# Dense weights split once into DRAM, gate's input normalized once, no POOL in the dense part, and the denominator's floor as a positive part on ScalarE

## The reference

```python
decay = exp(-exp(w)) * (0.5 + 0.5 * tf)          # per channel and batch
ek = exp(min(k, 30)); ekv = ek * v                # k and v are both the side input
nf, df = scan(ekv), scan(ek)                      # a = a * decay + in, forward
nb, db = the same, backward
euk = exp(min(u + k, 30))
num = nf + nb - ekv + euk * v
den = df + db - ek + euk
out = sigmoid(r) * (num / max(den, 1e-8)) * (0.8 + 0.2 * tf)

x = x + (out0(x) @ (weight * scale).T + bias)     # layer 0
c = out1(x)                                       # layer 1
flat = rmsnorm(c) * norm_w
top 4 of softmax(flat @ router_w.T), renormalized
routed = sum over the 4 of weight * (silu(flat @ w1g) * (flat @ w1u)) @ w2   # per expert
shared = (silu(flat @ sg) * (flat @ su)) @ sd
x = x + c + routed + shared
```

## Time and profile before

| | |
|---|---|
| three runs | 5500.07, 5501.99, 5503.63 us |
| profiled execution | 5515.08 us |
| its span | 5513.1 us, 61940 instructions |
| TensorE busy (PE) | 4469.8 us, 81% |
| VectorE busy (DVE) | 3139.4 us, 57% |
| ScalarE busy (ACT) | 1907.9 us, 35% |
| POOL busy | 1923.7 us, 35% |
| moved by DMA | 649.34 MB, mean 118 GB/s |

### The profile page before, as it was taken

The page is one execution under the profiler, slowest core; times in us unless marked ns, Lnnn a source line. Parts: engine busy times, 40 slices in busy tenths (PEclk is TensorE's granted clock), DMA queues, the critical chain, the costliest instruction groups (busy, mean ns, idle before and its releaser), DMA issues.

```text
span 5513.1 us, 61940 instructions
## 1 busy us (share of the span) xinstructions
PE 4469.8 (81%) x19471; PEld 3552.8 (64%) x19473; DVE 3139.4 (57%) x2812; ACT 1907.9 (35%) x2587; POOL 1923.7 (35%) x1350
## 2 busy tenths in 40 slices
PE   0036786868777787997459999999999999999998
PEld 0014555655555565765348888878878887888887
DVE  8889898988989896445222323434343214324232
ACT  2234444434444444442212223333343214223232
POOL 0023748475656657554721111111111111111111
PEclk9998888989888888998779999999999999999999
DMA  1123342424333334345433444545564435445352
GB/s 59 53 84 99 108 137 106 145 96 134 109 125 113 116 118 136 119 132 75 135 82 104 107 107 117 180 123 175 151 194 148 107 61 175 122 105 149 89 163 57
DMA packets 248186, 649.34 MB, mean 118 GB/s; under 512 B 44720, under 2 KB 110704, under 8 KB 223472
## 3 DMA queue, kind: packets, MB, share of 16 engines
q1 hardware_dynamic: 200224, 489.21, 26.0%
q0 software_dynamic: 47824, 158.43, 13.9%
HBM read 500.69 MB, written 146.87 MB: 117 GB/s over the span
## 4 chain that ended last, share of the span: by engine, by line
PE 53%; issue 2%; POOL 2%; DVE 1%; DMA 1%; ACT 0%; DVEq 0%; POOLq 0%; ACTq 0%; SPq 0%
PE ps L1273 30%; PE ps L1287 15%; PE ps L1174 4%; PE ps L1254 2%; POOL slots_dram L477 2%; PE ps L1262 1%; DMA slots_dram<-work 1%; PE ps L1192 0%; PE ps L1190 0%; DMA work<-slots_dram 0%; POOL halves L212 0%; DVE work L890 0%; DVE work L887 0%; DVE work L886 0%; POOL work L223 0%
## 5 line engine op out<-in xcount | busy, mean ns | idle before, releaser
L1174 PE MATMUL ps<-halves 128*128 128x512 f32 x6144 | 1606.3, 424 | 713.0 <-POOL halves L257 352.3
L1174 PEld LDWEIGHTS ps<-halves 128*128 128x128 f32 x6144 | 1249.5, 205 | 1066.7 <-issue 439.1
L1273 PE MATMUL ps<-halves 128*128 128x512 f32 x7152 | 1745.6, 397 | 27.5 <-DVE halves L1102 22.1
L1273 PEld LDWEIGHTS ps<-halves 128*128 128x128 f32 x7152 | 1328.9, 189 | 300.9 <-DVE halves L1102 24.3
L212 POOL TENSOR_TENSOR halves<-work,halves 128x1024 fp32r<-128x1024 f32 x239 | 694.9, 2909 | 675.7 <-ACT halves L598 675.4
L1287 PE MATMUL ps<-halves 128*128 128x512 f32 x3576 | 835.0, 389 | 1.3 <-DVE halves L1112 1.3
L1287 PEld LDWEIGHTS ps<-halves 128*128 128x128 f32 x3576 | 671.4, 188 | 140.5 <-DVE halves L1112 1.5
L1097 DVE TENSOR_TENSOR halves<-ps,halves 128x1024 fp32r<-128x1024 f32 x150 | 183.7, 1225 | 876.1 <-ACT halves L696 876.1
L459 POOL COPY add_idx<-work 128x1 int32 x149 | 27.0, 181 | 1692.1 <-DVE work L1118 1692.1
L1102 DVE TENSOR_TENSOR halves<-work,halves 128x1024 fp32r<-128x1024 f32 (+1 forms) x320 | 440.3, 1435 | 109.8 <-ACT halves L705 109.8
L696 ACT ACTIVATE halves<-ps 128x1024 fp32r<-128x1024 f32 x150 | 153.9, 1026 | 960.7 <-PE ps L1273 849.3
(11 more groups left out here) (163 smaller groups left out, 4582.0 us busy)
## 6 DMA issues: line engine op xcount, KB each, us to landing
work<-expert_w SPq DMA_DIRECT2D x192, 1024.0 KB, 5.5
work<-shared_w SPq DMA_DIRECT2D x256, 512.0 KB, 4.4
work<-side_t SPq DMA_DIRECT2D x33, 512.0 KB, 3.4
work<-x_t SPq DMA_DIRECT2D x33, 512.0 KB, 4.1
gated_dram<-work SPq DMA_DIRECT2D x32, 512.0 KB, 3.0
ratio_dram<-work SPq DMA_DIRECT2D x32, 512.0 KB, 2.9
work<-gated_dram SPq DMA_DIRECT2D x64, 256.0 KB, 2.7
work<-x_t SPq DMA_DIRECT2D x64, 256.0 KB, 3.2
```

What stands on the lines that cost most here:

```text
L1174: last = pe.matmul(bank(k % 4), w[k % 2][:, c * P:(c + 1) * P], op[:, part], start=(c == 0 and w is piece_hi and op is hi), stop=(c == CB ...
L1273: last = pe.matmul(ps_h[:, a * 512:a * 512 + 512], xp[:, xk * P:(xk + 1) * P], wp[:, rhs], start=(xk == 0 and xp is xhi and wp is whi), st ...
```

## The change

- Units 0 to 7's time also carries a split of the 32 weight pieces: SP loads four a unit, ScalarE writes the high part, TensorE computes piece minus high part in PSUM by two fp32 products (identity by piece, negative identity by high part), ScalarE copies it out as the low part, and SP stores both to `split_dram` (1 MB a piece). The eighth group runs behind unit 6, ahead of unit 7, without a unit of its own; then SP waits for all stores and loads the first three pieces.
- A product loads both parts as two 512 KB halves (each with the high and low part of four blocks of the contraction), in four slots, three pieces ahead. There is no split of weights in the halves.
- C1 is kept for all eight blocks. The sum of squares comes at step `step_l(o)` + 1. R is made at step 16, and Z = C1 x norm weight x R for all eight blocks there, with its split, transposes and logits; gate's and up's outputs need no factor then, nor do the experts. Rows are stored by one DMA of 2 MB per half.
- The low parts of z, c and the activation are made by VectorE; POOL keeps only fills, entries, gathers and adds.
- In the unit: the numerator's forward scan comes before the denominator's backward scan; the two edge products go to ScalarE; the floor becomes `Relu(den - low)` on ScalarE, and `low` is added back as the bias of Ln and in the first refining step.

The diff, cut to its core (SP's waits of the input loads, the declarations of tiles and the routing's index changes are left out):

```diff
+SLOTS = 4
+AHEAD = SLOTS - 1
...
-        def with_halves(eng, unit, fill, tail, loop_q=UNITS_PER_HALF):
+        def with_halves(eng, unit, fill, tail, alone, weights=lambda: None):
             with eng.Fori(0, 2 * UNITS_PER_HALF - 1) as u:
-                unit(u, nothing, alone=True)
+                unit(u, lambda i: alone(u, i))
+            last = 2 * UNITS_PER_HALF - 1
+            for i in range(FILLS_PER_UNIT):
+                alone(last, i)
+            weights()
             unit(2 * UNITS_PER_HALF - 1, lambda i: fill(-1, STEPS - FILLS_PER_UNIT + i, first=False, prev=False, next_=True))
...
+            def load_piece(h, k, step):
+                for j in range(2):
+                    wait(sp, "chunk" if j == 0 else "product", h * STEPS + (k - SLOTS + 1))
+                    sp.dma_start(piece[k % SLOTS][j].bitcast(i32), split_dram[(2 * step + j) * P:(2 * step + j + 1) * P, :])\
+                        .then_inc(piece_sem[k % SLOTS][j], 16)
...
+            def alone(u, i):
+                m = i // 2
+                if i % 2 == 0:
+                    sp.wait_ge(s["split_pe"], u * 4 + (m + 1))
+                    sp.dma_start(raw_w[m], shared_w[ds((u * 4 + m) * P, P), :]).then_inc(raw_sem[m], 16)
+                else:
+                    sp.wait_ge(s["split_lo"], u * 4 + (m + 3))
+                    sp.dma_start(split_dram[ds((u * 4 + m) * (2 * P), 2 * P), :].rearrange("(j p) c -> p j c", p=P),
+                                 split_w[m].bitcast(i32).rearrange("p (j c) -> p j c", j=2)).then_inc(split_sem[m], 16)
+            def weights():
+                for m in range(4):
+                    sp.wait_ge(split_sem[m], 8 * 16 + 1)
+                for k, i in first_half[:AHEAD]:
+                    load_piece(0, k, i)
...
-                if not final(h) or i <= FIRST_RANK:
-                    low_halves(pool, h, i, first, prev, next_)
...
-            split_piece_lo(pool, 0, 0)
-            with_halves(pool, unit, fill, lambda: None)
+            fill(HALVES - 2, 2, first=False, prev=True, next_=True)
+            fill(HALVES - 1, FIRST_RANK + 1, first=False, prev=True, next_=False)
...
+                def edges(l):
+                    at = ds(u + l * BLOCKS, 1)
+                    sc.wait_ge(s["h_fwd"], u * 2 + l + 1)
+                    sc.activation(edge_in[:, 0:1], F[:, SEQ - 1:SEQ], ACT.Copy, scale=edge[:, at]).then_inc(s["h_edge"], 1)
+                    sc.wait_ge(s["nf"], u * 2 + l + 1)
+                    sc.activation(edge_in[:, 1:2], G[:, SEQ - 1:SEQ], ACT.Copy, scale=edge[:, at]).then_inc(s["n_edge"], 1)
...
                 def inverse(l):
+                    sc.wait_ge(s["h_all"], u * 2 + l + 1)
+                    sc.activation(F, F, ACT.Relu, bias=neg_low[:, at]).then_inc(s["den"], 1)
                     sc.wait_ge(s["den"], u * 2 + l + 1)
-                    sc.activation(G, H, ACT.Ln).then_inc(s["g_ln"], 1)
+                    sc.activation(N, F, ACT.Ln, bias=low[:, at]).then_inc(s["g_ln"], 1)
                     sc.wait_ge(s["g_ln"], u * 2 + l + 1)
-                    sc.activation(G, G, ACT.Exp, scale=-1.0).then_inc(s["g_inv"], 1)
+                    sc.activation(N, N, ACT.Exp, scale=-1.0).then_inc(s["g_inv"], 1)
...
-            def split_piece(h, k):
+            def alone(u, i):
+                m = i // 2
+                if i % 2 == 0:
+                    sc.wait_ge(raw_sem[m], (u + 1) * 16)
+                    sc.wait_ge(split_sem[m], u * 16 + 1)
+                    sc.activation(split_part(m, 0), raw_w[m].rearrange("p (j c) -> p j c", j=2), ACT.Copy).then_inc(s["split_hi"], 1)
+                else:
+                    sc.wait_ge(s["split_pe"], u * 4 + (m + 5))
+                    sc.activation(split_part(m, 1), ps[m % 2][:, :].rearrange("p (j c) -> p j c", j=2), ACT.Copy)\
+                        .then_inc(s["split_lo"], 1)
...
+            def normalize(h):
+                ve.wait_ge(s["sums"], h * CB + CB)
+                ve.tensor_scalar(SQ, SUM_BANK, 1.0 / CH, 1e-6, ALU.mult, ALU.add).then_inc(s["mean"], 1)
+                ve.wait_ge(s["r_exp"], h + 1)
...
+                ve.scalar_tensor_tensor(R, SG, 1.5, R, ALU.add, ALU.mult).then_inc(s["r_set"], 1)
+                for o in range(CB):
...
+                    ve.scalar_tensor_tensor(Z[o % 2], C1[o], nrm[:, o:o + 1], R, ALU.mult, ALU.mult).then_inc(s["z"], 1)
+                    if o:
+                        split_z_lo(h, o - 1)
+                split_z_lo(h, CB - 1)
...
+            with pe.Fori(0, 2 * UNITS_PER_HALF) as u:
+                for m in range(4):
+                    pe.wait_ge(s["split_hi"], u * 4 + (m + 1))
+                    pe.wait_ge(s["split_lo"], u * 4 + (m + 1))
+                    for j in range(2):
+                        part = slice(j * HALF, (j + 1) * HALF)
+                        pe.matmul(ps[m % 2][:, part], ident[:, :], raw_w[m][:, part], start=True, stop=False)
+                        last = pe.matmul(ps[m % 2][:, part], neg_ident,
+                                         split_w[m][:, 2 * j * HALF:(2 * j + 1) * HALF].bitcast(f32), start=False, stop=True)
+                    last.then_inc(s["split_pe"], 1)
...
+            def square_sums(h, o):
+                pe.wait_ge(s["sq"], h * CB + (o + 1))
+                pe.matmul(SUM_BANK, ones[:, :], SQ, start=(o == 0), stop=(o == CB - 1)).then_inc(s["sums"], 1)
...
-                        if i == step_l(o) + 2:
-                            by_token(h, o)
+                        if i == step_l(o) + 1:
+                            square_sums(h, o)
...
+                    if i == 2 * CB - 1:
+                        for o in range(CB):
+                            by_token(h, o)
```

More of the change, by code:

```diff
@@ L305, in _ @@
                 sp.sem_inc(s[name], 1)
+            for done in split_sem:
+                sp.sem_inc(done, 1)
+            sp.sem_inc(s["split_pe"], 4)
+            sp.sem_inc(s["split_lo"], 2)
             sp.dma_start(ww[:, :], w_all).then_inc(s["cond_in"], 16)
@@ new lines, in _, with next_piece, load_cl @@
+            first_half = [(k, i) for i, k in products(0, True)]
+            def next_piece(h, k, first, next_):
+                ahead = k + AHEAD
+                if ahead < STEPS - CB:
+                    load_piece(h, ahead, dict(first_half)[ahead] if first else ahead + CB)
+                else:
+                    load_piece(h, ahead, ahead - (STEPS - CB) if next_ else step_d(ahead - (STEPS - CB)))
+            def load_cl(h, c):
+                rows, cols = half_rows(h, c)
+                if c < 2:
+                    wait(sp, "c1", (h - 1) * CB + (CB - 2 + c + 1))
+                else:
+                    wait(sp, "c_lo", h * CB + (c - 1))
+                sp.wait_ge(s["gated_out"], ((h // 2) * CB + (c + 1)) * 16 + 1)
+                sp.dma_start(RL[c % 2], gated_dram[rows, cols]).then_inc(rl_sem[c % 2], 16)
@@ L379, in store_out, with unit @@
                 sp.dma_start(to, RS.rearrange("p (t c) -> p t c", c=P)).then_inc(s["o_out"], 16)
-            def unit(u, fill, alone=False):
+            def unit(u, fill):
                 fill(0)
@@ L407, in _ @@
             load_x(0)
-            for k, src in first_half[:2]:
-                load_piece(0, k, src)
-            with_halves(sp, unit, fill, tail)
+            with_halves(sp, unit, fill, tail, alone, weights)
             def load_weights(j):
@@ L584, in unit @@
                 fill(3)
+                fill(4)
+                edges(1)
                 euk(1)
-                fill(4)
                 fill(5)
@@ L614, in out_copy, with rows_copy @@
                 sc.activation(RS, OUT_BANK, ACT.Copy).then_inc(s["o_copy"], 1)
+            def rows_copy(h, o):
+                sc.wait_ge(s["z_tr"], h * CB + (o + 1))
+                sc.activation(ZROWS[:, :, o * P:(o + 1) * P], Z_BANK.rearrange("p (t c) -> p t c", t=HT), ACT.Copy)\
+                    .then_inc(s["z_copy"], 1)
             def fill(h, i, first, prev, next_):
+                if prev and i == 0:
+                    act_hi(h - 1, CB - 1)
                 if not before_all(h):
-                    if any(i == a for a, _ in products(h, first)):
-                        split_piece(h, number(i, first) + 1)
                     for o in range(CB):
@@ L709, in silu @@
                 sc.wait_ge(s["a_tr"], g * 2 + 1)
-                apart(sc)
-                sc.activation(act[:, a * 256:a * 256 + 256], ps_h[:, a * 512:a * 512 + 256], ACT.Silu,
-                              scale=gains[:, ds(g + GT, 1)]).then_inc(s["silu_done"], 1)
+                sc.activation(act[:, a * 256:a * 256 + 256], ps_h[:, a * 512:a * 512 + 256], ACT.Silu).then_inc(s["silu_done"], 1)
             def split_act(g, a):
@@ L1069, in fill @@
+                if next_:
+                    for c in range(CB):
+                        if i == STEPS - CB + c:
+                            split_c_lo(h + 1, c)
                 if final(h, HALVES - 2) and i == 0:
@@ L1164, in product @@
```

(15 more changed lines are left out.)

485 lines of the change are left out of this document (213 added, 272 removed).

## The result

| | median | lowest to highest | ratio to before |
|---|---|---|---|
| before | 5502.81 us | 5500.07 to 5504.36, 4 runs | |
| after | 5616.16 us | 5613.68 to 5618.67, 4 runs | 1.0207, 95% interval 1.0189 to 1.0224 |

The change costs 113 us; 5434 with a range of 5320 to 5545 was predicted. The profiled execution of after took 5613.68 us, span 5612.0.

A forecast was written before the change was run, and what follows sets the result against it. VectorE was taken to bound halves 1 to 5. Terms 133 + 72 - 182 - 30 - 30 - 7.5 - 24 = -68.5 took the profiled 5515.08 to 5446.6; less 13.1 for the median, 5434 us, range 5320 to 5545.

The forecast's parts named there:

- the walk through the queues in halves 1 to 5: Halves 1 to 5, queues followed unit by unit: 262 us a half against 298.4, -182 in all.
- two squares behind inverses: Steps 0 to 7 of a half: two squares queued behind inverses on ScalarE, three cold products, 62.0 us.
- C1 at 9.8: Steps 8 to 15: C1 done 9.8 us after VectorE starts reading the fifth lin product, the square at 12.2.
- two sums and 14 products to 96: Half 6, its first two products already done: this stretch ends at 96 us; the half takes 211 against 241.3, -30.
- Rival 1: Halves: handshake on the squares and late 1 MB pieces cost more, 285 us a half, total +66, 5568 us; chance 0.19.
- Rival 2: Halves: scans fall in with the waits, VectorE's pace of 235 us a half, total -216, 5286 us; chance 0.12.
- Rival 3: Units 0 to 6: splits hide beside units at 42 to 44 us, loads running ahead, total 5308 us; chance 0.05.
- The units beside splits: Units 0 to 6 with four serial weight splits each: 61.6 instead of 42.1 us a unit, +133 in all.
- Unit 6 with the eighth group and unit 7: Before the halves: unit 61.6 us, then eighth weight group 73.9 and unit 7 47.8, together 121.7 instead of 49.4, +72.
- The routing: Half 7: starts 143 us in against 147.0 and takes 37.5 instead of 41 us, -7.5.
- the wait of rows 8: Before the puts: second slot fill landed 24 us after entries were ready; emptying slots earlier removes it, -24.
- The floor: Scan units: Relu on ScalarE frees 64 x 0.75 = 48 us of VectorE; taken alone the move would be 24 us worse.

The follow-up runs named there:

- four edits: Changed kernel with sums one step later, a group's four loads together, ScalarE's high part of the next input first, floor back on VectorE: 5133.78 us, ratio 0.9331.

## Why the prediction was wrong

**The step that failed** is the walk through the queues in halves 1 to 5, at the sentence "the sum of squares now follows one product earlier, and TensorE stands until ScalarE's square of it". The mechanism was named; it was followed at too few places. Its four parts, in pairs that need no common boundary: steps 24 to 31 and 0 to 7 were put at 67.0 + 62.0 = 129 and took 54.1 + 91.3 = 145; steps 8 to 15, 65.3 against 68.9; steps 16 to 23, 66.4 against 68.5. That is 22 us a half over the walk's 260.7. The prediction had "two squares behind inverses" there; the trace has the read of the first lin product behind three scans, its sigmoid behind the exponential and sigmoid of x, and 12.7 us of TensorE standing. That is a chain of the kind that was worked out for the fifth lin product, at a place where it was not looked for. The second part is the order on VectorE. The prediction let C1 follow the sigmoid at once ("C1 at 9.8"), but in the code the read of the down product stands before it, and so the sum always comes after that product. The run with C1 first has the order that was assumed, and it parts the two: its steps 8 to 15 take 65.2 us, the predicted 65.3, while its steps 24 to 31 and 0 to 7 stay some 10 us over the 129. So about 10 us a half are the order on VectorE, and about 10 stay in the stretch with the chain ahead of the first sum.

**It was then not carried on.** For half 6 the prediction took "two sums and 14 products to 96": seven pairs without a stop. The pairs took 14.6 and 16.2 us in turn, and these steps 129.2; the rest of the half took 110.9 where 115 was said. Half 7 has the same pairs: ranking begins 167.5 in where 143 was said. Half 0 took 267 against 251. These are the +29, +24 and +16 of the account. With C1 first, 22 us are gone from each of halves 6 and 7 and none from half 0. With the sums later, half 6 took 211.1, the predicted 211, though by two misses that cancel (99.1 against 96, 112.0 against 115); ranking began 144.8 into half 7; half 0 took 235 and halves 1 to 5 took 247 each, both under the forecast, which had counted some stops. That the halves lost their time at the sums is shown by this one edit. The window is half 6 of that run:

```profile
2047.30:2258.40 211.10, 199.87 (x848) 154.72 (x849) 89.72 (x120) 61.69 (x99) 0.76 (x1) 0.96 0.68 221
```

**Rival 1** was this mechanism, "each lin product waits for VectorE, ScalarE, and a cold TensorE in turn", with its point of decision at 276 us a half; the half took 281.6. Its price, 285, was near; its total of +66, against +99 in the spans, missed because it left halves 6 and 7 at the forecast. Its second part, a late weight piece, did not occur: the products waited 1.2 us for `split_dram` in five halves. Its chance of 0.19 was too low, and the reason given against it (VectorE's sum leaves 69 us) argued from a busy sum, not from the order.

**Rival 2**, halves at VectorE's pace (235), is a length that the halves come near to once the orders are mended: 247 with the sums later, 239 with four edits. That VectorE sets them there is not shown; with four edits TensorE is busy 210 us of a half and VectorE 202.

**Rival 3**, the splits hidden, was rightly put down by the order on SP, and the run with the loads ahead shows that this order was all but 3 us a unit of what stood against it.

**What was right.** The units beside splits: 62.7 against 61.6, with VectorE waiting for the inverse (87.6 us in twelve waits in units 0 to 5) and ScalarE for the load:

```profile
ACT halves L631 <- DMA plain<-shared_w: 173.7, 23, 9.6
DVE work L871 <- ACT work L607: 87.6, 12, 10.0
```

Unit 6 with the eighth group and unit 7 took 182.8 where 61.6 + 121.7 was said. The scans at 2.28 in the halves, from 3.24: the slowdown was POOL's, as the section on specifications in the Trainium skill's "GPSIMD Engine Reference" has it, and none of it stayed when POOL was idle, though TensorE was about as busy in the halves as before and the DMAs busier (a share of 0.55 against 0.36). What this alone is worth in the length of a half no run shows, since TensorE's stops now set it. The routing: 37.0 from 2657.4 to the entries, against 37.5. The slots were emptied at 2612 and 2639, ahead of the entries at 2694.41, and the puts began at once, so the wait of rows 8 is gone:

```profile
2612.28 3.49 POOL L510 DMA_DIRECT2D slots_dram<-work  x1 [0.32 <-POOL work L505]
2639.22 3.44 POOL L510 DMA_DIRECT2D slots_dram<-work  x1 [23.45 <-issue]
...
2695.78 1.06 POOL L494 DMA_INDIRECT slots_dram<-put_val,put_idx  x1 [0.90 <-POOL put_val L490]
```

The experts changed by 4.

**The floor.** The prediction priced it by the queues and not by itself, and in a unit of the changed kernel it freed VectorE's time as said. But nothing waited for VectorE there. The rule for relu and max in the Trainium skill's "ScalarE: Activation LUTs", Rules for kernel authors, prefers VectorE. By the durations in the rows the move would then cost 25 us (64 x 0.39; the prediction wrote 24); back on VectorE the floor gave 4 and 10, the sign of the rule at a size that these runs hardly tell from none.

**Sums that do not come out.** Unit 7 was put at 47.8, but its terms add up to 48.4; nothing hangs on it.

## What to carry to other kernels

Where an engine is relieved, write down for each instruction of the new bound what stands ahead of its inputs on the other queues, and do it at every place where the pattern occurs, the first of a round and the rounds without other work too: in half 6 seven stops of 2 us, one of 7.6 and the slower work behind some of them cost 30 us, as much as the whole gain that was expected there. A small reduction on TensorE whose input takes a round trip through two other engines belongs as many products later as the round trip is long; moving one line here turned a loss of 2% into a gain of 2.7%. A load that stands behind a store of the result before it, on one queue, makes a serial chain of what the engines could do side by side.

## What the runs showed of the hardware

Behind a stop of 2.0 to 2.2 us on TensorE a product often took 7.3 to 7.7 us at a granted share near 0.8, against 6.05 behind a sum without a stop; but in half 6 of after this held for every other stop of 2.04 us only, and the products between took 6.03. Behind stops of 1.3 to 1.4 us (C1 first) it took 6.02 to 6.06. With the sums later, steps 8 to 15 moved 260 GB/s at a DMA share of 0.76 and a granted clock of 1.00, 49.1 us of TensorE work in 50.8. Two fills of the slots from POOL were issued 26.9 us apart, 23.45 of them idle with nothing that the profile shows; in before the idle time was 26.05; what holds the second back was not tried.
